# Six-layer decoder stack on one core: the late gating's counts, one-hots and origins in another form, two joints in another order

## What is computed

```python
x = x + L0_attn(layernorm(x))            # attention, then a dense MLP
x = x + L0_xattn(layernorm(x), ctx)      # cross attention, 16 heads of 16
x = x + L0_ffn(layernorm(x))             # attention, then 8 experts of width 512, best 2, and a shared one
x = x + L1_attn(layernorm(x))            # retention: decayed scores, no softmax, norm per head
x = x + L1_xattn(layernorm(x), ctx)      # cross attention, band of 64
x = x + L1_ffn(layernorm(x))             # 16 experts of width 128, best 2, and shared ones

def _gate(xf, gate_w, gate_b):           # L1_ffn, T = 2048 tokens
    orig = softmax(xf @ gate_w.T)
    scores = orig + gate_b
    sg = scores.reshape(T, 4, 4)
    group_scores = top_k(sg, 2)[0].sum(-1)
    keep = one_hot(top_k(group_scores, 2)[1], 4).sum(1) > 0
    _, idx = top_k(where(keep[:, :, None], sg, -inf).reshape(T, 16), 2)
    return take_along_axis(orig, idx, 1), idx
```

## Time and profile before

| | |
|---|---|
| median of 3 runs | 1462.07 us |
| lowest and highest | 1457.41 and 1466.78 us |
| time of the profiled execution | 1464.77 us |
| its span, first to last instruction | 1462.9 us |
| PE busy | 1298.5 us (89%) |
| DVE busy | 867.4 us (59%) |
| POOL busy | 705.6 us (48%) |
| ACT busy | 571.1 us (39%) |
| mean granted clock of PE | 0.953 |

### The profile page before, as it was taken

One profiled execution on the slowest core, in us unless ns is written; L12 is line 12 of the kernel. 1 busy time (PEld: TensorE's weight loads), 2 busy tenths in 40 slices (PEclk: granted clock), 3 DMA queues, 4 the chain that ended last, 5 costly groups with the idle time before them and its releaser, 6 DMA issues.

```text
span 1462.9 us, 33803 instructions
## 1 busy us (share of the span) xinstructions
PE 1298.5 (89%) x12132; PEld 1045.0 (71%) x12132; DVE 867.4 (59%) x2050; ACT 571.1 (39%) x1272; POOL 705.6 (48%) x949
## 2 busy tenths in 40 slices
PE   5999979988999999979889999959998999818897
PEld 4666647876777777758889999846765777617776
DVE  4888743337888888736512121158875778773346
ACT  2555535523444455643222222214443555413331
POOL 5566632017667466630223333237784556427426
PEclk9999968998999999989999999979999999958999
DMA  6000000020000000000298999630000000028964
GB/s 252 2 2 0 2 1 30 1 86 16 13 15 5 2 16 15 16 16 1 80 338 314 334 325 328 245 137 30 0 16 9 25 28 26 16 92 284 316 189 144
DMA packets 47370, 137.79 MB, mean 94 GB/s; under 512 B 6925, under 2 KB 29646, under 8 KB 41104
## 3 DMA queue, kind: packets, MB, share of 16 engines
q1 hardware_dynamic: 32944, 110.37, 21.4%
q0 software_dynamic: 7536, 19.67, 4.4%
q10 hardware_dynamic: 6768, 6.16, 1.2%
HBM read 119.54 MB, written 17.56 MB: 94 GB/s over the span
## 4 chain that ended last, share of the span: by engine, by line
PE 61%; DVE 14%; DMA 10%; issue 8%; POOL 5%; ACT 1%; DVEq 0%; SPq 0%; POOLq 0%; ACTq 0%
PE ps L1159 11%; PE ps L1018 8%; PE ps L967 7%; PE ps L1292 7%; PE ps L1066 5%; DMA back_of<-w_odd 4%; DMA row_in<-rows_of,from_u 4%; PE ps L1304 3%; PE ps L1035 3%; PE ps L1044 3%; DVE negmax L1734 3%; PE ps L911 2%; PE ps L958 2%; PE ps L1073 2%; PE ps L993 2%
## 5 line engine op out<-in xcount | busy, mean ns | idle before, releaser
L1292 PE MATMUL ps<-hT,w_tile 128*128 128x128 f32 x1624 | 199.9, 278 | 8.4 <-DMA w_tile<-in_w_f 7.4
L1292 PEld LDWEIGHTS ps<-hT,w_tile 128*128 128x128 f32 x1624 | 190.6, 194 | 12.6 <-issue 7.1
L1358 ACT ACTIVATE probsT_all<-ps 128x1024 f32<-128x1024 f32 x128 | 131.1, 1024 | 158.3 <-PE ps L967 158.3
L1734 DVE TENSOR_REDUCE negmax<-ps 128x8 f32<-128x1024 f32 x128 | 155.9, 1218 | 54.2 <-PE ps L967 53.9
L967 PE MATMUL ps<-qe,kf 32*128 32x256 f32 x1280 | 152.9, 386 | 0.0
L967 PE MATMUL ps<-ke,qf 32*128 32x256 f32 x1024 | 143.6, 398 | 0.0
L747 POOL TENSOR_SCALAR eps_sum<-mv 128x1 f32<-128x1 f32 x112 | 25.4, 227 | 201.0 <-DVE mv L1671 169.4
L967 PEld LDWEIGHTS ps<-qe,kf 32*128 32x128 f32 x1280 | 110.4, 189 | 4.9 <-issue 2.7
L2255 DVE TENSOR_TENSOR h_in<-ps,act_sb 128x512 f32<-128x512 f32 x39 | 27.0, 691 | 143.3 <-PE ps L1292 143.3
L1066 PE MATMUL ps<-probsT_all,va 128*32 128x128 f32 x2560 | 104.4, 281 | 6.1 <-ACT probsT_all L1358 4.4
L691 POOL DMA_INDIRECT back_of<-be,to_u x39 | 39.4, 1010 | 144.7 <-DVE be L2268 144.7
(11 more groups left out here) (266 smaller groups left out, 3226.8 us busy)
## 6 DMA issues: line engine op xcount, KB each, us to landing
w_tile<-in_w_f SPq DMA_DIRECT2D x39, 1536.0 KB, 9.3
w_tile<-in_w_f SPq DMA_DIRECT2D x47, 385.0 KB, 7.3
back_of<-w_odd ACTq DMA_DIRECT2D x47, 128.0 KB
ctxT<-in_ctxT SPq DMA_DIRECT2D x32, 128.0 KB, 2.1
rows_of<-nv SPq DMA_DIRECT2D x32, 128.0 KB, 1.7
w_even<-in_w_att SPq DMA_DIRECT2D x3, 1024.0 KB, 7.2
y_back<-back_of SPq DMA_DIRECT2D x6, 512.0 KB, 5.0
x_all<-in_x SPq DMA_DIRECT2D x4, 512.0 KB, 10.6
```

The costliest lines, as they stand in the source:

```text
L1292: last = mm(ps[:, 2 * which + at.two, fc * P:(fc + 1) * P], w[:, col:col + P], rowT[:, at.two, c, :], start=c == 0, stop=c == KC - 1)
L1358: nc.scalar.activation(half_of(probsT_all, half), ps[:, 2:4].rearrange("p b n -> p (b n)"), ACT.Exp, scale=HD ** -0.5).then_inc(S["probs"], 1)
L1734: nc.vector.tensor_reduce(m, ps[:, 0:2].rearrange("p b (h k) -> p (b h) k", h=HB), AX.X, ALU.max, negate=True).then_inc(S["s_max"], 1)
```

## The change

It has three parts.

**Gating of MOE1.** `place` is no longer called for MOE1: `late_ranks` lets PE sum the `chosen` tiles themselves, group by group, into the same bank. DVE reads counts and ranks where PE wrote them, without the two copies. `part` is f32 (for MOE0 as well), and `hot_rows` becomes 16 operations with a per-partition scalar in place of one with two tensors. `slot_tile` is multiplied by 128 times the number of the tile (`steps_of`) in place of the number, 24 of the 32 columns by DVE and 8 by POOL, so that `late_origins` adds both products into one bank and one DVE operation makes `from_u`. The parts of the gating of group 2 stand one tile earlier.

**MOE0's joint.** `gate_moe0(15)`, which waits for the origins, stands behind `add` of group 2. The second weight buffer is now where `y_back` and the low halves of the dense input lie, and is loaded when the last `h_done` is in; the third and fourth wait for PE's last `down`, not for the last `add`.

**Start of the retention.** `normalise` of the first tile stands ahead of `combine_next`, and the third tile is combined and normalised in the step of the second.

```diff
+LATE_BLOCKS = 24
...
-        part = sb("part", [P, 2, 2 * NT], bf16)
+        part = sb("part", [P, 2, 2 * NT])
...
-            return (w_tile0, w_tile1, w_tile2, w_tile3)[b][:, 0:f_cols(f)]
+            return (w_tile0, w_back, w_tile2, w_tile3)[b][:, 0:f_cols(f)]
...
+                    elif j == 1:
+                        sp.wait_ge(S["h_done"], units("h_done", f, F_EXPERTS[f] - 1, GROUPS - 1, D_CHUNKS[f]))
                     else:
-                        sp.wait_ge(S["acc_done"], units("acc_done", f, F_EXPERTS[f] - 1, GROUPS - 1, GT))
+                        sp.wait_ge(S["down_out"], units("down_out", f, F_EXPERTS[f] - 1, GROUPS - 1, GT))
...
+                def late_origins():
+
+                    n, out = F_TILES[f], ps[:, 0, 0:F_TILES[f]]
+                    pe.wait_ge(S["tile_nth"], 2)
+                    for i in range(2 * NT):
+                        if i in (0, NT):
+                            pe.wait_ge(S["row_hot"], 4 if i == 0 else 6)
+                        if i == LATE_BLOCKS:
+                            pe.wait_ge(S["tile_grp"], 3)
+                        mm(out, slot_row[:, i], tile_in[:, i, 0:n], start=i == 0, stop=False)
+                        last = mm(out, slot_row[:, i], slot_tile[:, i, 0:n], start=False, stop=i == 2 * NT - 1)
+                    last.then_inc(S["hot_out"], 1)
+
+                def late_ranks():
+
+                    place_ = ps[:, 4, D:2 * D].rearrange("p (t e) -> p t e", e=16)
+                    mm(place_, ones_bf[:], chosen[:, 0:1].to_broadcast([P, NT, 16]), start=True, stop=False)
+                    for g in range(GROUPS):
+                        pe.wait_ge(S["scan_done"], 2 + g)
+                        blocks = range(g * GT, (g + 1) * GT)
+                        for t in blocks:
+                            count = mm(ps[:, 5, D:D + 16], ones_bf[:], chosen[:, FRONT + t], start=t == 0, stop=t == NT - 1)
+                        for t in blocks:
+                            if t + 1 < NT:
+                                mm(place_[:, t + 1:NT], ones_bf[:], chosen[:, FRONT + t:FRONT + t + 1].to_broadcast([P, NT - 1 - t, 16]),
+                                   start=False, stop=False)
+                        rank = mm(place_[:, blocks[0]:blocks[0] + GT], tri_bf[:], chosen[:, FRONT + blocks[0]:FRONT + blocks[0] + GT],
+                                  start=False, stop=g == GROUPS - 1)
...
+            def rooted(at):
+
+                if 3 not in at or at[3].l == RET and at[3].t == 2:
+                    return []
+                tile = at[3]
+                return [tile, tiles_of(RET, 2)] if tile.l == RET and tile.t == 1 else [tile]
...
+                for tile in first[1:]:
+                    variance(tile)
+                    combine(MOE0, tile.t + 1)
+                    normalise(tile)
...
-                    if gate_piece(at) == (GROUPS - 2, 3):
-                        gate_moe1(GROUPS - 2, 4)
-                    gate_moe1(*gate_piece(at))
+                    group, k = gate_piece(at)
+                    for part_ in ((0,), (1, 2), (4,), (3,))[k] if group == GROUPS - 2 else (k,):
+                        gate_moe1(group, part_)
...
-            def hot_rows(k):
-
+            def hot_rows(f, k):
+
+                if f == MOE1:
+                    for i in range(k * NT, (k + 1) * NT):
+                        last = ts(slot_row[:, i], iota_all[:], part[:, 1, i:i + 1], None, ALU.is_equal)
+                    last.then_inc(S["row_hot"], 1)
+                    return
...
+                if step_ == 4 and f == MOE1:
+                    dve.wait_ge(S["tile_nth"], 2)
+                    for a, b, last in ((0, NT, NT), (NT, LATE_BLOCKS, LATE_BLOCKS - NT)):
+                        table = slot_tile[:, a:b, 0:m]
+                        tt(table, table, steps_of[:, 0:last].unsqueeze(2).to_broadcast([P, last, m]), ALU.mult).then_inc(S["row_hot"], 1)
+                    hot_rows(f, 1)
...
+                    if f == MOE1:
+                        ts(from_u[:, 0:m], ps[:, 0, 0:m], -1.0, 0.0, ALU.add, ALU.max).then_inc(S["from_done"], 1)
+                        return
...
-                        if f == MOE0:
+                        if f == MOE0 and fc + 1 < n or f == MOE0 and g + 1 < GROUPS:
                             gate_moe0(q)
...
                             add(e, p, g - 1)
+                            if f == MOE0 and g + 1 == GROUPS:
+                                gate_moe0(GROUPS * n - 1)
...
-                    place(MOE1, hot[:], sc[:])
```

91 lines of the change are left out of this document (55 added, 36 removed).

## The result

The changed kernel ran in 1449.20 us (median of 6 runs, 1446.55 to 1452.46), the kernel before in 1467.36 beside it (6 runs, 1457.41 to 1475.28). The ratio is 0.9894, interval 0.9866 to 0.9921; the forecast was 1451.2, a ratio of 0.9926 to the median of 1462.07 that it started from. The profiled execution took 1449.05 us (span 1447.2) against 1464.77: -15.7.

| stretch | before | after | difference | forecast |
|---|---|---|---|---|
| start to the end of the last `h_tmp` of MOE0 | 712.06 | 711.13 | -0.9 | 0 |
| from there to `up` of block 1 (term A) | 22.77 | 16.47 | -6.3 | -5.5 |
| from there to `h_in` of block 2 | 3.88 | 3.77 | -0.1 | 0 |
| `h_in` of the 2nd to the 39th block | 212.11 | 209.56 | -2.6 | 0 |
| last `h_in` to the first `combine` | 9.92 | 9.63 | -0.3 | 0 |

The account below looks back on a forecast made before the run. The prediction took PE at its own pace to bound most of the kernel (61% of the chain). Its terms, -5.5 - 1.5 - 2.2 - 1.7 = -10.9 us off the median of 1462.07, gave 1451.2, range 1444.5 to 1458.5.

Parts of the forecast that it names:

- term A: MOE0's joint: adds ahead of the wait for the origins and earlier weights bring `up` of block 1 forward, -5.5 us.
- The sum: Whole kernel: -5.5 - 1.5 - 2.2 - 1.7 = -10.9 us, taken off the median of 1462.07, gives 1451.2.
- B: Retention's start: first tile's `u` ahead of a `combine`, third tile's `u` two DVE steps earlier; -1.5 us.
- C2: MOE1's gating, from `chosen` to `from_u`: shorter chain, 16 pointer operations at 0.20 us per half; -1.7 us.
- its high end of -6.2: MOE0's joint: if rows come quicker than in MOE1, PE's own 722.8 binds and the gain is 6.2 us.
- everything carried through: Whole kernel: the forecast in which all savings reach the end, 1451.2 us; chance 0.52.
- rivals 1 and 2: MOE0's routed blocks; the first: rows or weights set the pace and swallow the joint's gain, only 5.4 left, 1456.7; chance 0.16.
- Rival 2: MOE0's routed blocks: row waits shrink as weights stand further ahead, up to 5.9 us more, 1445.3 to 1451; chance 0.16.
- So PE's wait of 3.15 us at 976.37 ends, but not all of it is gained: Retention's start: PE no longer waits for the third tile's `u`; put at -1.5 us, 3 being the whole wait.
- C1: MOE1's gating, behind the last tile's logits: group 2's parts move one tile earlier; -2.2 us, or -1.5 without the cast's surplus.
- the cast's surplus: MOE1's gating of group 2: extra time of an 8-column cast that took 1.33 us, which may go; -2.2 with it, -1.5 without.
- the estimate from the Trainium skill: MOE1's `slot_row`: a bf16 `tensor_scalar` at four elements a cycle, 0.17 us an operation, some -2.7 from `chosen` to `from_u`.

Follow-up runs that it names:

- after_old_g2: The changed kernel with the parts of MOE1's gating of group 2 back one tile later; one run, 9.22 us from the last logits to `chosen`.

## Why the prediction was right, step by step

- **The sum: right, in part by luck.** The four terms come to -11.1 in the two traces, -10.9 forecast; but B fell short by 1.4 and A and C2 went over by 1.7, so that the misses cancel. The other 4.6 of the 15.7 us lie where nothing was forecast (see the last point). The time came out 2 us from the forecast, but the sum was taken off the median of three runs (1462.07), and the kernel before took 1467.36 in the comparison: against the one the change is -12.9, against the other -18.2.
- **Term A: right, mis-sized by 0.8,** and 0.1 beyond its high end of -6.2. Every step is in the trace: no wait at `down`, clock at 1.00, no wait for `w_tile`. It was taken as -5.5 with 0.3 deducted for weights beside the first rows, and another 0.3 because these were to come after PE was free. There was no such cost: the first turn came at 722.42, 0.5 after the last add, `up` of block 0 1.79 after that add (as before), and `up` of block 1 3.87 behind block 0 (4.0 reckoned).
- **"everything carried through": right, against rivals 1 and 2.** The 39 blocks gave nothing of the 6.3 us back. Rival 2 had the sign of the -2.6 in them, but the experiments leave most of that to scatter. With it the ratio came out just under 0.99 (0.9894), where the prediction had put a chance of 0.22.
- **Term B: the step that failed** is "So PE's wait of 3.15 us at 976.37 ends, but not all of it is gained". The 0.4 of the first `u` and the 1.9 at the third tile's projection are there. Then the prediction stopped, one tile too early. The next thing that PE waits for is `decay` (3.47 us), which comes only 1.1 us earlier than before (21.24 us after the first `combine` against 22.38), and behind that wait the clock falls and takes 1.4; the sum had no term for either. Of 1.5 forecast, 0.1 lie between the two traces and about 0.6, not proved, in the mean.
- **C1: right** (-2.1 against -2.2), with the cast's surplus, as `after_old_g2` shows.
- **C2: right in mechanism, mis-sized by 0.9.** `slot_row` starts at 7.2 (7.27 reckoned). An operation costs 0.17, not 0.20: the estimate from the Trainium skill ("VectorE: DVE Perf Modes", The perf-mode tier table) was the nearer one, as was its -2.7. That one is in part luck, since it had no price for POOL's product beside them, which is 0.6 on DVE's side (0 to 0.8 was allowed, on POOL's). The prediction set 3.2 against the 2.24 in the earlier trace rows and drew nothing from it.
- The rest of the difference (-0.9 before the joint, -2.6 in the 39 blocks, -0.3 behind them, -0.8 in MOE1's blocks) lies where the change does nothing, or where no gain of it is shown.

## What to carry to other kernels

When a wait of the bounding engine is removed, follow that engine past the next two or three operations, to the point where it meets the old chain again; here a gain of 1.9 us was gone 14 us later, the larger part of it with the engine's clock. An operation is well placed in a gap in which its engine waits anyway, and moving it "first" can cost more than it brings. And a table that feeds a matmul is best handed over in pieces: four increments in place of one gave 1 us, while what comes behind (rows, weights) has to be free to use it.

## What the runs showed of the hardware

- 16 DVE operations of 128 bf16 columns with one pointer scalar ran at 0.17 us each; one of 2048 columns with two tensors, one of them repeated, took 2.24 us, or 0.14 per 128 columns.
- A POOL product of 376 bf16 columns took 0.83 us beside such pointer operations and slowed them by 0.6 us; beside two-tensor operations it took 4.73 us and didn't slow them.
- A DVE cast of 8 columns took 1.08 to 1.33 us beside POOL memsets of 1024 and 512 columns (five traces), and 0.17 without them (nine).
- The first indirect fetch of rows in MOE1 took 3.43 to 3.50 us from its issue to the first use at DMA shares from 0.22 to 0.54 (ten traces; an eleventh 3.72 at 0.36), and 4.40, 4.94 and 4.77 at 0.61, 0.69 and 0.73.
- The same code showed a second fall of PE's granted clock behind a wait of about 2 us in some executions and not in others, at a price of 1.4 us between two attentions.
